# The last seven edge tiles of a pass fetched row by row by SyncE and ScalarE

## The reference, cut to what matters

```
# L0: four steps
m = (embedding @ W_msg.T + b_msg).reshape(n, 4, 128)
r = segment_sum(m[src, etype], dst);  embedding = gru(r, embedding)
# L1
pe  = relu(edge_w @ pos_w1) @ pos_w2
msg = pe * x[src] + x[src];  s = segment_sum(msg, dst) / max(count, 1)
out = relu(batchnorm(concat([x, s]) @ sage_w + sage_b)) + x
# L2
msg = h[src] @ W_msg.T + b_msg + edge_embed[edge_type]
h = gru(segment_sum(msg, dst), h)
# L3: attention over the edges (q[dst] * (k[src] + e), softmax per dst,
#     (v[src] + e) * alpha summed per dst), gate, graph norm, feed forward
```

## Time and profile before

| | us |
|---|---|
| median of 3 runs | 4272.25 (4272.07 to 4273.12) |
| the profiled execution, its time | 4261.16 |
| the profiled execution, its span | 4259.2 |

### The profile page before, as it was taken

The page is one execution under the profiler, slowest core; times in us unless marked ns, Lnnn a source line. Parts: engine busy times, 40 slices in busy tenths (PEclk is TensorE's granted clock), DMA queues, the critical chain, the costliest instruction groups (busy, mean ns, idle before and its releaser), DMA issues. The chain is left out here.

```text
span 4259.2 us, 50937 instructions
## 1 busy us (share of the span) xinstructions
PE 2837.7 (67%) x12039; PEld 2147.9 (50%) x12040; DVE 1817.0 (43%) x4892; ACT 925.5 (22%) x3024; POOL 2749.5 (65%) x2882
## 2 busy tenths in 40 slices
PE   6555585655855558666677787766556766665697
PEld 3444444444444444444446676644445455555484
DVE  5222252222522225444463333432222666667885
ACT  3111131111311113111122332321111211111233
POOL 4777767777677776777737777457776377775100
PEclk9777797777977779777878999977777888887798
DMA  5221222212212122222212121112121154543240
GB/s 175 53 52 52 52 88 52 52 52 52 88 52 52 52 53 88 53 52 52 52 31 68 52 53 53 33 51 53 52 52 48 59 158 153 158 153 120 97 160 15
DMA packets 141572, 308.75 MB, mean 72 GB/s; under 512 B 48723, under 2 KB 63258, under 8 KB 140986
## 3 DMA queue, kind: packets, MB, share of 16 engines
q0 software_dynamic: 95040, 208.45, 18.2%
q1 hardware_dynamic: 46458, 99.48, 6.7%
HBM read 246.11 MB, written 61.63 MB: 72 GB/s over the span
## 5 line engine op out<-in xcount | busy, mean ns | idle before, releaser
L642 POOL DMA_INDIRECT ring<-m_tab,idx x1564 | 1488.0, 951 | 542.1 <-issue 474.2
L1709 PE MATMUL ps<-oh,ring 128*128 128x256 f32 (+1 forms) x2816 | 881.5, 477 | 470.7 <-DMA ring<-m_tab,idx 373.8
L1709 PE MATMUL ps<-nodes,ring 128*128 128x256 f32 (+1 forms) x2768 | 867.5, 477 | 479.4 <-DMA ring<-m_tab,idx 361.3
L762 ACT ACTIVATE ring<-ring 128x128 f32 x2346 | 506.2, 295 | 2232.6 <-DMA ring<-m_tab,idx 1555.8
L1709 PEld LDWEIGHTS ps<-oh,ring 128*128 128x128 f32 x2816 | 635.8, 249 | 615.0 <-issue 508.9
L1709 PEld LDWEIGHTS ps<-nodes,ring 128*128 128x128 f32 x2768 | 625.5, 249 | 623.0 <-issue 520.4
L642 POOL DMA_INDIRECT ring<-x_tab,idx x782 | 740.5, 947 | 247.9 <-issue 237.1
L1145 DVE TENSOR_SCALAR oh<-iota,dl 128x256 f32<-128x256 f32 x1200 | 367.5, 376 | 927.3 <-PE ps L1709 926.9
L1145 DVE TENSOR_SCALAR nodes<-iota,dl 128x256 f32<-128x256 f32 x1176 | 359.2, 375 | 825.0 <-PE ps L1709 825.0
L642 POOL DMA_INDIRECT ring<-kv_tab,idx x416 | 404.8, 973 | 133.7 <-issue 126.4
L1709 PE MATMUL ps<-wpad,rts 128*128 128x128 f32 x832 | 160.8, 372 | 181.9 <-DVE pw L1450 181.9
(11 more groups left out here) (283 smaller groups left out, 2716.9 us busy)
## 6 DMA issues: line engine op xcount, KB each, us to landing
ve_dr<-pw SPq DMA_DIRECT2D x52, 512.0 KB
ring<-ve_dr SPq DMA_DIRECT2D x52, 512.0 KB, 3.3
ring<-m_tab,idx POOLq DMA_INDIRECT x1564, 2.5
m_tab<-ring SPq DMA_DIRECT2D x75, 256.0 KB, 2.1
ring<-x_tab,idx POOLq DMA_INDIRECT x782, 2.5
ring<-kv_tab,idx POOLq DMA_INDIRECT x416
nodes<-in_xT SPq DMA_DIRECT2D x2, 1600.0 KB, 13.9
kv_tab<-nodes SPq DMA_DIRECT2D x25, 128.0 KB, 1.7
```

Of the source, the lines that this page charges most:

```text
L642: pool.indirect_dma_start(rows[:, j, :], None, table, bass.IndirectOffsetOnAxis(ap=idx[:, wave * WV + j:wave * WV + j + 1], axis=0)).then_ ...
L762: ins = nc.scalar.activation(ring_flat[:, ds(r[j], P)], rows[:, j, :], ACT.Copy)
L1709: return T.matmul(o, lhsT, rhs, start=start, stop=stop, skip_group_check=True)
```

## The change

The constants first. A pass now has 48 whole waves (`FULL`) of 384 tiles (`NEAR`) that GpSimd gathers, and seven tiles (`FAR`) that come row by row: 896 plain DMAs of 512 bytes, 512 of them from SyncE and 384 from ScalarE, nine after each of its first 43 waves. The address of a row is read from SBUF into a register of the engine. The seven tiles have a place of their own, `far_place`, in the tile `rec`. In L1 ScalarE issues none; its three tiles are gathered by GpSimd into the same place, behind wave 42. The engines that use the tiles take the waves at the end in the order 44, 45, 46, 48, 47, so that the wave which lands last is now a whole one, cut into five and three tiles. VectorE computes the byte offsets of the rows (two small operations), and SyncE turns them into rows of numbers on one partition by way of DRAM, before the first pass; ScalarE waits for this before its first copies.

```
-M_FIRST = 4
+M_FIRST = 5
+FULL = TILES // WV
+NEAR = FULL * WV
+FAR = TILES - NEAR
+SP_TILES, ACT_TILES = 4, 3
+ACT_ROWS = 9
+ROW = 4 * D
...
-        END_HALVES = {M_WAVES - 1: (4, 6), M_WAVES: (0, 1), M_WAVES + 1: (5,)}
+        far_place = rec_flat[:, 3600:3600 + FAR * D].rearrange("p (t d) -> p t d", d=D)
+        TAIL_WAVES = (FULL - 4, FULL - 3, FULL - 2, FULL, FULL - 1, M_WAVES, M_WAVES + 1)
+        END_HALVES = {FULL - 1: (2, 3), FULL: (4, 5), M_WAVES: (0, 1), M_WAVES + 1: (None,)}
...
+        def far_arrived(eng, k):
+            for b in range(4):
+                eng.wait_ge(x_sp[b], (k + 1) * X_SP)
+            if isinstance(k, int) and k == PASS_L1:
+                eng.wait_ge(x_l1, 16 * ACT_TILES)
+            else:
+                for b in range(4):
+                    eng.wait_ge(x_ac[b], (k if after_l1(k) else k + 1) * X_AC)
+
+        def fetch_rows(eng, which, table, rows, t0, first, n, sems):
+            flat = table.rearrange("n d -> (n d)").bitcast(U8)
+            r = load_rows(eng, which, rows, first, n, (table.shape[0] - 1) * ROW)
+            for j in range(n):
+                t, q = t0 + (first + j) // P, (first + j) % P
+                eng.dma_start(far_place[q:q + 1, t, :].bitcast(U8),
+                              flat[ds(r[j], ROW)].rearrange("(a n) -> a n", a=1)).then_inc(sems[(first + j) % 4], 16)
...
+            def sp_rows(table, j):
+                for q in range(0, SP_TILES * P, 2 * WV):
+                    fetch_rows(sp, mybir.EngineType.SP, table, sp_rowno[j], 0, q, 2 * WV, x_sp)
+
             first_table(m_rows)
             sp.dma_start(wpad_flat, a["wpad"]).then_inc(s_wpad, 16)
-            for s in range(1, STEPS):
-                table(s, m_rows, 512)
+            sp.wait_ge(s_dv, DV["x_b1"])
+            for j in range(2):
+                sp.dma_start(xi_dr[j].rearrange("(k p) -> p k", p=P), x_bytes[j],
+                             allow_slow_non_contiguous=True).then_inc(xi_st, 16)
+            sp.wait_ge(xi_st, 32)
+            for j in range(2):
+                row = xi_dr[j].rearrange("(a n) -> a n", a=1)
+                sp.dma_start(sp_rowno[j], row[:, 0:SP_TILES * P]).then_inc(xi_ld, 16)
+                sp.dma_start(ac_rowno[j], row[:, SP_TILES * P:FAR * P]).then_inc(xi_ld, 16)
+            sp.wait_ge(xi_ld, 64)
+            sp.wait_ge(s_dv, DV["x_ka"])
+            sp.wait_ge(s_pe, PE["dT"])
+            for s in range(STEPS):
+                if s:
+                    table(s, m_rows, 512)
+                for b in range(RING):
+                    sp.wait_ge(mt_dma[b], (s + 1) * (16 * MT_SLOTS[b]))
+                sp_rows(m_tab, 0)
...
-                waves, deep, slots = (WAVES, RING, SLOTS) if single(k) else (M_WAVES, DEPTH, TILES)
+                waves, deep, slots = (WAVES, RING, SLOTS) if single(k) else (FULL, DEPTH, NEAR)
...
+                    if k == PASS_L1 and g == FULL - 6:
+                        for t in range(SP_TILES, FAR):
+                            pool.indirect_dma_start(
+                                far_place[:, t, :], None, table,
+                                bass.IndirectOffsetOnAxis(ap=idx[:, NEAR + t:NEAR + t + 1], axis=0)).then_inc(x_l1, 16)
...
+            def act_rows(table, j, first):
+                n = min(ACT_ROWS, ACT_TILES * P - first)
+                if n > 0:
+                    fetch_rows(act, mybir.EngineType.Activation, table, ac_rowno[j], SP_TILES, first, n, x_ac)
+
+            def keep_tiles(k, table, j0):
+                for p, g in enumerate((*range(FULL - 4), *TAIL_WAVES[:5])):
+                    n = tiles_of(g)
                     r = load_kept(act, kept_at, mybir.EngineType.Activation, first_slot(g), n)
-                    arrived(act, k, i, u, g)
-                    act.wait_ge(kept, k * M_WAVES + i * DEPTH + u + 1)
+                    arrived(act, k, p // DEPTH, p % DEPTH, g)
+                    act.wait_ge(kept, k * M_WAVES + p + 1)
                     for j in range(n):
-                        if n == M_LAST and j == M_FIRST:
+                        if g == FULL - 1 and j == M_FIRST:
                             last_arrived(act, k)
-                        keep(r, j, wave_rows(g, u), j == n - 1)
-
-                split_turns(act, wave)
+                        keep(r, j, wave_rows(g, p % DEPTH), j == n - 1)
+                    act_rows(table, j0, p * ACT_ROWS)

             act.wait_ge(s_dv, DV["x_ka"])
+            act.wait_ge(s_pe, PE["dT"])
+            act.wait_ge(xi_ld, 64)
```

More of the change, by code:

```diff
@@ L91, in load_kept, with load_rows @@
         skip_runtime_bounds_check_because="the column of one of 20 places for tiles")[1]
+def load_rows(eng, which, xrow, start, n, hi):
+    return eng.bass.values_load_multi_w_load_instructions(
+        xrow[0:1, start:start + n], engines=[which], min_val=0, max_val=hi,
+        skip_runtime_bounds_check_because="the row numbers that the gathers use, below the table's length")[1]
 def load_both(pe, row, wave):
@@ L138, in in_first @@
 def in_first(wave):
-    return M_FIRST if wave == M_WAVES - 1 else WV
-IN_SLOT = [16 * sum(in_first(wave) for wave in range(s, M_WAVES, DEPTH)) for s in range(DEPTH)]
+    return M_FIRST if isinstance(wave, int) and wave == FULL - 1 else WV
+IN_SLOT = [16 * sum(in_first(wave) for wave in range(s, FULL, DEPTH)) for s in range(DEPTH)]
 def landed(k, s, i, n=WV):
@@ L282, in build @@
         kept = sem("kept")
+        xi_st = sem("xi_st")
+        xi_ld = sem("xi_ld")
+        x_l1 = sem("x_l1")
+        x_sp = [sem(f"x_sp{i}") for i in range(4)]
+        x_ac = [sem(f"x_ac{i}") for i in range(4)]
         border = sem("border")
@@ L416, in split_turns, with after_l1 @@
         def split_turns(eng, body):
-            with eng.Fori(0, LOOPED) as i:
+            with eng.Fori(0, LOOPED - 1) as i:
                 for u in range(DEPTH):
                     body(i, u, i * DEPTH + u, WV)
-            for u in range(P_REST):
-                body(LOOPED, u, LOOPED * DEPTH + u, tiles_of(LOOPED * DEPTH + u))
+            for p, wave in enumerate(TAIL_WAVES):
+                body(LOOPED - 1, p, wave, tiles_of(wave))
         def wave_rows(wave, u):
+            if isinstance(wave, int) and wave == FULL:
+                return far_place
             return slot(wave % DEPTH if isinstance(wave, int) else u)
+        X_SP, X_AC = (n * P // 4 * 16 for n in (SP_TILES, ACT_TILES))
+        def after_l1(k):
+            return isinstance(k, int) and k >= PASS_L1
+        def far_arrived(eng, k):
[13 more added lines that the diff above has]
+                              flat[ds(r[j], ROW)].rearrange("(a n) -> a n", a=1)).then_inc(sems[(first + j) % 4], 16)
         def arrived(eng, k, i, u, wave):
@@ L431, in arrived @@
                 eng.wait_ge(gat[u], landed(k, u, i))
+            elif wave == FULL:
+                far_arrived(eng, k)
             else:
@@ L473, in whole_turns @@
                 turn(i, [i * DEPTH + u for u in range(DEPTH)])
-            turn(LOOPED - 1, list(range((LOOPED - 1) * DEPTH, M_WAVES)))
+            turn(LOOPED - 1, TAIL_WAVES[:5])
         def y_st(c, w):
@@ L586, in _ @@
                 sp.dma_start(dst, src).then_inc(s_w2 if j else s_w1, 16)
+            for c in range(2):
+                sp.wait_ge(ln_dma[c], LN_DMA(1, c))
+            sp_rows(x_tab[0], 1)
             rows_out(1)
+            for c in range(2):
+                sp.wait_ge(ln_dma[c], LN_DMA(2, c))
+            sp_rows(x_tab[1], 1)
             table(STEPS, kv_rows, 2 * D)
@@ L644, in gathers @@
                             bass.IndirectOffsetOnAxis(ap=idx[:, wave * WV + j:wave * WV + j + 1], axis=0)
-                        ).then_inc(gat_end if not single(k) and wave == M_WAVES - 1 and j >= M_FIRST else gat[u], 16)
+                        ).then_inc(gat_end if not single(k) and wave == FULL - 1 and j >= M_FIRST else gat[u], 16)
+                    if k == PASS_L1 and g == FULL - 6:
[3 more added lines that the diff above has]
+                                bass.IndirectOffsetOnAxis(ap=idx[:, NEAR + t:NEAR + t + 1], axis=0)).then_inc(x_l1, 16)
             def norm(ln):
@@ L1047, in _ @@
                                           ALU.logical_shift_left))
+            after("i_4")
+            step("x_b0", V.tensor_scalar(x_bytes[0], idx4[:, NEAR:TILES], 9, None, ALU.logical_shift_left))
             th = small[:, 32:32 + EXTRA]
@@ L1341, in messages @@
                 for u, wave in enumerate(waves):
-                    final = isinstance(wave, int) and wave == M_WAVES - 1
+                    final = isinstance(wave, int) and wave == FULL - 1
                     for hf in range(2):
```

31 lines of the change are left out of this document (19 added, 12 removed).

## The result

The changed kernel takes 4243.98 us (median, 4241.86 to 4248.12), the kernel before 4272.68 us on the same chip. The ratio is 0.9927, 95% interval 0.9907 to 0.9947: it is 0.73% faster, 28.7 us, and the interval lies clear of 1. The forecast was 4243 us, 29 us faster. The profiled execution took 4242.07 us (span 4240.3), 19.1 us less than the one before.

A forecast was written before the change was run, and what follows sets the result against it. Gathers alone set the pace in L0 and L2; L1 is bound by its own cycle. Gains of 33.4 us less 1.5 for collisions and 3 for the start gave 28.9, say 29: median 4272.25 to 4243, range 4232 to 4254.

The forecast's parts named there:

- Seven gathers less, 8.75 us a pass: GpSimd's path: seven of 391 gathers removed at 1.25 us each in five passes, 43.75 us in all, nothing in L1.
- A tail with less cover: End of each pass: far tiles delay the borders, leaving gains of 7.1, 7.1, 6.8, 6.0 and 6.4, together 33.4 us.
- The bound for the lower clock: Pass end: TensorE's matmuls take double the 0.226 us through the tail, 6.8 us more a pass, leaving next to nothing.
- ScalarE's and SyncE's rows: no cost: Row issues, 0.48 us each with the gap, hide in ScalarE's 8.4 us of waiting and SyncE's 480 us.
- The point from which ScalarE is late: ScalarE's wave in the passes: the next wave's copies come late once a row costs 0.8 us.
- The two register loads: ScalarE in each wave: two loads of row addresses, about 0.55 us, within 7.1 us of work out of 10.0.
- The cover: ScalarE's 8.4 us of waiting in each wave was to hide the work of its row transfers.
- Collisions 1.5 us: Gathers beside 896 small DMAs a pass: lengthened by 1.5 us in all, bounds 0 to 7.2.
- Start 3 us: Before the first pass: ScalarE waits for row numbers, costing 3 us; between no cost and 9 us late.
- Layer 1, 0 us: L1: three gathers behind wave 42 land wave 46 at 2714.2 against its use at 2714.6, so no cost.
- if the fit fails: L1: if the three added gathers make wave 46 land too late, the cost is 0 to 4 us.
- the split in 16 pieces: DMA queues: each 512-byte row cut into 16 pieces of 32 bytes, about 175 us more of each engine's time a pass.

The follow-up runs named there:

- the first repeat: The changed kernel run again with no edit, against the kernel before: 4235.82 us, ratio 0.9927.
- the second repeat: The changed kernel run a third time with no edit, against the kernel before: 4235.5 us, ratio 0.9928.

## Why the prediction was right, step by step

*Seven gathers less, 8.75 us a pass: right.* From its first to its last gather GpSimd took 482.1, 481.2 and 481.3 us in step 1 instead of 490.1. Undoing this part alone costs 44.5 us where the sum had 43.75, but that the two agree so well is luck: 38.0 us of it by the table lie in the five passes that the sum counted, and 8.1 in layer 1, which it put at nothing.

*A tail with less cover: right where the work is simple, priced too low in step 3.* The borders began at T+12.91, predicted T+13.0. The passes gained 5.9, 7.0 and 6.8 us in steps 0 to 2, predicted 7.1, 7.1, 6.8; in step 0 GpSimd's first wait alone scatters by 3.6. Step 3 gained 2.3 instead of 6.0: wave 47's one-hots wait for wave 46's matmuls, as the program's rule of two waves in flight says, which I had not followed for this wave (0.5 us), wave 50's come 0.5 us later than I had them, and three border tiles ran at the lower clock (1.5 us). That is 2.5 of the 3.7 us; the rest I can't place. Layer 2 gained 3.7 instead of 6.4, but that may be chance: the kernels with fewer rows and with rows twice into SBUF, whose layer 2 has the same order, took 570.5 and 570.6 us there against the changed kernel's 571.5 to 576.1, which is 7.0 us less than before. The bound for the lower clock was in the range; its value in the sum was zero. With the far wave one place earlier step 3 gains 7.7 us and layer 2 6.4.

*ScalarE's and SyncE's rows: no cost, right, and priced too high.* 0.32 us a row against 0.48 on ScalarE, 0.41 against 0.55 on SyncE. A mean between issues of far larger transfers was the nearest row, not a near one. The point from which ScalarE is late, 0.8 us, lies between what was measured: 0.66 us for two issues passed, 1.07 did not. The two register loads were priced too low instead: the one of nine values took 2.14 us and not 0.55, part of it while the copies still ran. The cover was wide enough for it.

*Collisions 1.5 us: none seen,* the lower end of the bounds: the gathers' median is 944 to 947 ns in every kernel with rows, and 944 also with the rows twice. *Start 3 us: nothing that can be seen.* GpSimd's wait there is 5.4 us in the mean before and 5.9 in the changed kernel, and scatters by more. ScalarE's 6.8 us late start was forecast (up to 9), but TensorE had run ahead meanwhile and ScalarE caught up, with a copy each 0.48 us instead of 0.86.

*Layer 1, 0 us: wrong by 3 to 4, of the 0 to 4 that were allowed "if the fit fails".* I had compared wave 46's landing with its use, four waves behind the three added gathers. The wave that waits is the first one behind them, 43, which has the least lead: it waited 7.18 us where 4.1 is normal, and 5.51 in the first repeat. In the second repeat it did not wait, since there the cycle came to it some 3 us later by itself, and the layer took as long all the same (511.7 us to the transposes). Without those gathers this stretch takes 507.4 to 510.8 us in four profiles, with them 511.2 to 515.2 in seven, and 518.0 with seven gathers there. (The table has only 1.9 us, since two of the changed kernel's three profiles had two slow pairs in the norm, and before's had three and four.) That the gathers cost time here is shown, the way by which they do is shown in part.

The sum put the cost of the start and of collisions too high by 4 to 5 us and that of step 3 and layer 1 too low by 6 to 8, so the errors offset each other in part. The profiled executions gained 23.5 us, and the medians 28.7 to 30.5. The mechanism is the one that was forecast; that the median hit 29 within 2 us is partly luck. Why the medians differ by more than the profiled executions stays open; the spread of single executions, up to 17 us in one set, may be enough for it.

Of the split in 16 pieces, which the prediction took from the Trainium skill, "DMA: Bandwidth & Descriptors", section "Why a DMA increments its semaphore by 16 and not by 1": this case shows that it goes by where the row is written. Into SBUF it did not happen, two packets a row on q10; the measurement decides. Into DRAM there were 32 packets a row, and there the issue costs 0.50 us. (The prediction's 175 us also stand for 32 packets a row; 16 pieces of one packet would give half.)

## What to carry to other kernels

Work that is taken off the pacing engine must still be done, and where it is put decides what is left of the gain: put it where the waiting engines still wait for a later landing, not between the last two. When a queue is given extra work in mid-stream, look at the first consumer behind it, which has the least lead, not at the last. Before many small transfers are spread over an idle engine, time one of them into the kind of memory that it will go to. A difference of a few ns between two profiles is a cause only when a second profile of each kernel repeats it.

## What was not expected of the hardware

A 512-byte row costs 0.21 us to issue into SBUF and 0.50 us into DRAM, with 2 and 32 packets, and rows into SBUF that alternate with rows into DRAM rise to 0.38 us. A register load of nine values took ScalarE 2.14 us in the median, against 0.55 for eight before and 1.23 for sixteen on SyncE. It is not the copies that still run when it starts: 55 of the 215 loads, with as many copies ahead of them, took less than 1 us. What decides it is not shown. The lines of these loads:

```profile
L104 ACTq TENSOR_LOAD <-cols_p x215: 947/2139/2180, 86.8 to 3217.5; - x108
L104 SPq TENSOR_LOAD <-cols_p x192: 1132/1232/1413, 73.3 to 2986.2; - x192
```

In the norm behind layer 1 TensorE's pairs of matmuls take 2.05 us at the lower clock and 1.1 at the higher, and the number of slow pairs, two to four in kernels that are alike there, moves the end by up to 4.7 us (47.3 to 52.0).

The 3 ns by which a gather was longer in the first profile of the changed kernel, 6 us over 1920 gathers, were that execution's own.
